# Semaphore head starts, filler products and the end of batch 0's scan in an eight-batch model kernel

## The reference, cut to what matters

```python
x = L0_attn_input_tensor                       # (8, 512, 128)
xn = _layernorm(x)
x = x + filter_0(xn) + moe_0(xn)
xn = _layernorm(x)
x = x + attention_1(xn) + moe_1(xn)
```

```python
u, res = split(xn @ in_proj_w.T)               # 256 channels each
u = silu(conv_b + 4-tap causal convolution of u)
dt, Bm, C = split(u @ x_proj_w.T)              # 8, 16 and 16 columns
delta = softplus(dt @ dt_proj_w.T + dt_proj_b)
h[t] = exp(delta[t] * A) * h[t-1] + delta[t] * Bm[t] * u[t]    # 16 states a channel
y[t] = sum over the states of h[t] * C[t]
m = ((y + u * D_skip) * silu(res)) @ out_proj_w.T
```

## Time and profile before

| | |
|---|---|
| median of 3 runs | 2461.3 us (2459.88 to 2467.54) |
| profiled execution, its own time | 2465.32 us |
| its span in the trace | 2463.2 us |
| mean granted TensorE clock | 0.904 |
| TensorE busy | 2038.7 us (83%) |
| VectorE busy | 1646.4 us (67%) |
| ScalarE busy | 1173.7 us (48%) |
| GpSimd busy | 958.8 us (39%) |

### The profile page before, as it was taken

One profiled execution on the slowest core, in us unless ns is written; L12 is line 12 of the kernel. 1 busy time (PEld: TensorE's weight loads), 2 busy tenths in 40 slices (PEclk: granted clock), 3 DMA queues, 4 the chain that ended last, 5 costly groups with the idle time before them and its releaser, 6 DMA issues.

```text
span 2463.2 us, 40604 instructions
## 1 busy us (share of the span) xinstructions
PE 2038.7 (83%) x12424; PEld 1295.3 (53%) x12424; DVE 1646.4 (67%) x2939; ACT 1173.7 (48%) x2703; POOL 958.8 (39%) x580
## 2 busy tenths in 40 slices
PE   4267888997899878998899888997789888988985
PEld 1033445664466545664466544664456644665564
DVE  3944786568865887658865788558866688644431
ACT  2223464345644466346643456345553456424631
POOL 1420583017810495007820387105840068303501
PEclk8567799988999999999999989999999889989997
DMA  2000012321213112321113112231123211132233
GB/s 105 0 18 0 27 46 71 117 78 38 89 66 111 57 46 69 112 91 46 60 67 122 63 48 79 78 101 58 42 69 116 85 46 56 69 127 74 73 114 112
DMA packets 82459, 175.18 MB, mean 71 GB/s; under 512 B 11448, under 2 KB 42560, under 8 KB 81984
## 3 DMA queue, kind: packets, MB, share of 16 engines
q1 hardware_dynamic: 78144, 164.05, 19.3%
q0 software_dynamic: 4096, 8.40, 1.1%
HBM read 123.71 MB, written 15.14 MB: 56 GB/s over the span
## 4 chain that ended last, share of the span: by engine, by line
PE 49%; DVE 17%; issue 15%; POOL 8%; ACT 5%; DMA 3%; SPq 1%; DVEq 0%; POOLq 0%; ACTq 0%
PE G L1049 5%; DVE HS L1564 4%; PE G L1065 4%; PE FM L1038 3%; DMA MW<-moe 3%; POOL Y L1998 3%; PE G L942 3%; PE G L953 3%; PE G L936 3%; PE FC L1026 2%; PE G L1087 2%; PE FM L906 2%; PE FC L1077 2%; POOL REG L2009 2%; POOL REG L2012 2%
## 5 line engine op out<-in xcount | busy, mean ns | idle before, releaser
L1564 DVE TENSOR_TENSOR_SCAN HS<-DA,D 128x1024 f32<-128x1024 f32 x128 | 351.0, 2742 | 15.0 <-ACT DA L1232 14.5
L1049 PE MATMUL G<-ident,REG 128*128 128x128 f32 x1280 | 242.9, 290 | 121.5 <-ACT SL L1361 79.4
L1998 POOL TENSOR_TENSOR Y<-Y,HC 128x1024 f32<-128x1024 f32 x114 | 280.4, 2460 | 144.7 <-DVE HC L1586 101.9
L2009 POOL TENSOR_TENSOR REG<-REG,cos_t 128x512 f32<-128x512 f32 x128 | 173.9, 1359 | 263.9 <-ACT REG L1334 263.7
L1049 PEld LDWEIGHTS G<-ident,REG 128*128 128x128 f32 x1280 | 149.3, 147 | 166.0 <-issue 147.4
L1038 PE MATMUL G<-REG 64*128 64x128 f32 (+3 forms) x768 | 221.4, 487 | 12.4 <-POOL REG L2012 11.3
L2012 POOL TENSOR_TENSOR REG<-REG 128x512 f32<-128x512 f32 x128 | 190.6, 1489 | 62.0 <-DMA REG<-ROT 54.9
L1350 ACT ACTIVATE REG<-G,maxes 128x128 f32<-128x128 f32 (+3 forms) x384 | 196.9, 513 | 25.8 <-DVE maxes L1865 24.9
L1232 ACT ACTIVATE DA<-DELTA,a_neg 128x511 f32<-128x511 f32 x256 | 180.9, 721 | 46.8 <-DVE HS L1564 46.7
L1865 DVE TENSOR_REDUCE maxes<-G 128x1 f32<-128x128 f32 (+3 forms) x384 | 165.6, 458 | 27.9 <-PE G L1041 27.9
L1559 DVE TENSOR_TENSOR D<-DU,FB 128x1024 f32<-128x1024 f32 x114 | 138.6, 1216 | 46.6 <-PE FB L796 43.5
(11 more groups left out here) (297 smaller groups left out, 4568.2 us busy)
## 6 DMA issues: line engine op xcount, KB each, us to landing
MW<-moe SPq DMA_DIRECT2D x120, 768.0 KB, 4.4
REG<-ROT SPq DMA_DIRECT2D x256, 128.0 KB
EW<-experts SPq DMA_DIRECT2D x16, 514.5 KB, 4.3
XG<-x_rows SPq DMA_DIRECT2D x8, 960.0 KB, 5.4
y_rows<-YO SPq DMA_DIRECT2D x120, 64.0 KB, 1.5
X<-xT SPq DMA_DIRECT2D x8, 256.0 KB, 5.9
W<-weights SPq DMA_DIRECT2D x1, 2048.0 KB, 9.4
REG<-xT SPq DMA_DIRECT2D x8, 256.0 KB, 2.6
```

Source lines behind the costliest of these rows:

```text
L1049: mm = pe.transpose(G[2][:, c * P:(c + 1) * P], PR[:, n % 2, c * P:(c + 1) * P], ident[:, :])
L1564: dve.tensor_tensor_scan(HS[:, :, :].rearrange("p h s -> p (h s)"), DA[:, n % 2, :, :].rearrange("p h s -> p (h s)"), D1[:, :, :].rearrang ...
L1998: pool.tensor_tensor(Y[:, :, :], Y[:, :, :], HC_EARLY if early else HC[:, n % 2, :, :], ALU.add).then_inc(y_add.sem, 1)
L2009: pool.tensor_tensor(rotated, rotated, cos_t[:, :], ALU.mult).then_inc(rope_d.sem, 1)
```

## The change

Four edits:
- SP raises only x_in's semaphore before the loads, the other 14 behind all ten first loads.
- TensorE raises three semaphores first (those that others wait for in their first step), and the 42 others in groups of 16, 16 and 10 behind steps p = 0, 1 and 2 of its front. VectorE does its four memsets before its 50 increments.
- Behind steps p = 3 to 10 TensorE multiplies the constants `avg` and `ones` 6, 2, 2, 2, 2, 4, 3 and 4 times into G[0]. Nobody reads the result, and nobody waits for these products.
- In batch 0 GpSimd does adds 0 to 14; the add of state 15 and the product with silu(res) are done by VectorE, behind its HC 15, with a wait for GpSimd's add 14. `front_end` stays in use for the other batches.

```diff
--- before.py
+++ after.py
@@ -564,8 +564,7 @@
 
         @block.sync
         def _(sp):
-            for s in by_sp:
-                s.head_start(sp)
+            x_in.head_start(sp)
             late = WEIGHTS["wq"][0]
             sp.dma_start(X[:, :], xT[0]).then_inc(x_in.sem, 16)
             for dst, src in ((conv_w[:, :, :], conv_rows.partition_broadcast(P)), (in_u, in_u_w), (ident[:, :], identity), (V_[:, :], vecs),
@@ -574,6 +573,10 @@
             for dst, src in ((W[:, 0:late], weights[:, 0:late]), (dt_lhs[:, :], dt_w), (causal_f, causal), (row_of_sb[:, :], row_of),
                              (row_bias[:, :], row_biases.partition_broadcast(P))):
                 sp.dma_start(dst, src).then_inc(s_const, 16)
+
+            for s in by_sp:
+                if s is not x_in:
+                    s.head_start(sp)
 
             sp.wait_ge(s_rows, 1)
             sp.dma_start(x_rows.rearrange("(p r) d -> p (r d)", p=P), REG[:, 0:4, :].rearrange("p k s -> p (k s)")[:, 0:MOE_TILES * D]).then_inc(s_rows, 16)
@@ -683,9 +686,16 @@
 
         @block.tensor
         def _(pe):
-            for s in by_pe:
+            first_waited = (n1.by_pe, dp_mm, r_mm)
+            others = [s for s in by_pe if s not in first_waited]
+            for s in first_waited:
                 s.head_start(pe)
             pe.wait_ge(s_made, 4)
+
+            def keep_warm(n):
+
+                for _ in range(n):
+                    pe.matmul(G[0][:, 0:P], avg[:, :], ones[:, :], start=True, stop=True)
 
             def bank(key, b, f):
 
@@ -1163,6 +1173,13 @@
                     elif p == 5:
                         pe.wait_ge(s_const, n_loads)
                     front_start(b, p, None)
+                    if p < 3:
+                        for s in others[16 * p:16 * (p + 1)]:
+                            s.head_start(pe)
+                    elif p < 11:
+                        keep_warm((6, 2, 2, 2, 2, 4, 3, 4)[p - 3])
+                for s in others[48:]:
+                    s.head_start(pe)
                 pe.wait_ge(s_made, 15)
                 for n in range(STATES):
                     front_b(b, n)
@@ -1426,12 +1443,12 @@
 
         @block.vector
         def _(dve):
-            for s in by_dve:
-                s.head_start(dve)
             dve.memset(avg[:, :], 1.0 / P).then_inc(s_made, 1)
             dve.memset(ones[:, :], 1.0).then_inc(s_made, 1)
             dve.memset(XN[:, 0:PAD], 0.0).then_inc(s_made, 1)
             dve.memset(DA[:, :, :, 0:1], 0.0).then_inc(s_made, 1)
+            for s in by_dve:
+                s.head_start(dve)
 
             def taps_made():
 
@@ -1943,6 +1960,14 @@
                     for part in range(3):
                         front_step(b, n, part, FB, FC)
 
+
+                dve.wait_ge(y_add.sem, y_add.at(b, STATES - 1))
+                dve.wait_ge(hc_mul.sem, hc_mul.at(b, STATES))
+                dve.tensor_tensor(Y[:, :, :], Y[:, :, :], HC[:, (STATES - 1) % 2, :, :], ALU.add).then_inc(y_add.sem, 1)
+                dve.wait_ge(y_add.sem, y_add.at(b))
+                dve.wait_ge(r_silu.sem, r_silu.at(b))
+                dve.tensor_tensor(Y[:, :, :], Y[:, :, :], SR[:, :, :], ALU.mult).then_inc(y_gate.sem, 1)
+
             def late():
 
                 dve.wait_ge(s_late, n_late)
@@ -2096,13 +2121,11 @@
                 front_skip(b)
                 front_du(b)
                 front_copy(b)
-                for n in range(STATES):
-                    if n + 1 < STATES:
-
-                        pool.wait_ge(scan_d.sem, scan_d.at(b, n + 2))
-                        pool.sem_inc(pool_passed, 1)
+                for n in range(STATES - 1):
+
+                    pool.wait_ge(scan_d.sem, scan_d.at(b, n + 2))
+                    pool.sem_inc(pool_passed, 1)
                     front_step(b, n)
-                front_end(b)
 
             def late():
```

## The result

The changed kernel takes 2450.19 us (median of 22 executions, 2425.95 to 2463.54), the kernel before beside it on the same chips 2460.59 us (22 executions, 2451.03 to 2473.97). The ratio is 0.9944 with the interval 0.9922 to 0.9966. It isn't the quotient of the two medians (0.9958); that of the two means lies within 0.0003 of it. Ratios leave out disturbed executions, one here (2463.54) and one of 2588.13 us in the first set with the fillers alone. On the median of 2461.3 us that the forecast started from, the ratio gives 2447.5 us (2442.1 to 2452.9). I had forecast 2454.3 with a range from 2449.9: the sign is right, the gain (13.8 us) is twice what I gave. Two more sets of the changed kernel, run later, gave 0.9956 and 0.9955, so the size isn't one lucky set.

What follows compares the result with a forecast made beforehand. The prediction took the start, front and scan of batch 0 as one serial chain, mostly TensorE and VectorE work plus issue time. Gains 4.1 + 2.2 + 1.0 - 0.3 = 7.0 us took 2461.3 to 2454.3 us, range 2449.9 to 2460.0.

Steps and rivals of the forecast that it cites:

- SP's order: Program start: 14 of SP's 15 increments move behind the loads, 0.9 us; X's load issued at 0.75, landed at 3.35.
- Rival 4: Program start: X lands at 6.65, so the start gains 1.2 us instead of 4.1; total 2457.2 us; chance 0.05.
- TensorE's and VectorE's order: Program start: first product at 3.4, mean subtracted at 5.95 instead of 10.02, VectorE being last; gain 4.1 us.
- Increments put off: Batch 0's front: TensorE's 42 postponed increments fit in its idle gaps and cost 0, with 0.9 us kept for the range.
- rival 3: Batch 0's front: increments wait for the products ahead of them, losing 0.9 us in two gaps; 2455.2 us; chance 0.10.
- End of the scan: Batch 0's scan: with last add and gate on VectorE, the `out_proj` product starts at 137.3 instead of 139.53; gain 2.2 us.
- Fillers: Batch 0's front: 0.3 us lost behind first taps, 1.0 gained by holding the clock for the second step-width product; net 0.7.
- rival 2: Batch 0's front: fillers hold nothing, second step-width product still takes 2.07 us; gain 6.0, total 2455.3 us; chance 0.17.
- Rival 1: First tap products of the front: clock rises sooner, up to 3.0 us more gain; total 2451.3 us; chance 0.20.
- The sum: Start, scan and front together: 4.1 + 2.2 + 1.0 - 0.3 = 7.0 us, moving everything from `out_proj` on earlier.

Runs made afterwards that it cites:

- the head starts alone: Kernel before with only the reordered increments (SP's 14, TensorE's 42, VectorE's memsets first), no fillers, scan end as before: 2458.35 us, ratio 0.999.
- cut kernels: Kernels shortened to batches 0 and 1, or 0 to 2, by leaving out the loop over later batches; with two batches the change gained 6.5 us in means.
- the cut to two batches: Kernel before, changed kernel, change without fillers and fillers alone, each with only batches 0 and 1; the change gained 6.5 us in means.
- neither cut: Two batches: fillers lowered the changed kernel's mean by 0.2 us, raised that of before by 0.3; three batches: 1024.79 us with fillers, 1022.1 without.

## Why the prediction was right and where it was wrong

**SP's order: right.** X's load went out at 0.81 (0.75 forecast) and landed at 3.61 (3.35), in 2.80 us. Rival 4, X late, is out.

**TensorE's and VectorE's order: right.** First product at 3.74 (3.4), subtraction at 5.93 (5.95), first taps at 15.85 (15.8). Which engine is last I had the wrong way round: 3.74 + 2.06 and 0.13 for the signal are 5.93, and with the product at 3.52 (the head starts alone) the subtraction follows at 5.71, so VectorE's increments end before that and not at 5.85, and TensorE sets the time. It cost nothing in the sum: the gain is 4.1 us, up to 4.4 in other executions.

**Increments put off: right.** The idle times of 2.98, 2.32 and 0.87 us are those of before to the hundredth; rival 3 is out.

**End of the scan: right.** 2.3 us, 2.2 forecast. VectorE added at 129.40 and gated at 130.66, and the centring of the next batch, pushed back to 131.80, made nobody wait.

**Fillers: the term had the wrong sign in the front.** I had +0.7, from a price of 0.3 us and a gain of 1.0. The price is 0.34 and 0.35 us in two pairs of traces, and can be more, as the second step-width product comes later against the clock's fall: from the subtraction to `out_proj` it is 126.1 to 126.5 us in the six traces with head starts, scan's end and fillers (cut kernels included) and 125.4 in the four with the first two alone. The gain isn't there: without fillers the second step-width product takes 1.12 to 1.22 us in six of seven traces of whole kernels (the first trace of before is the seventh), and with them it is slow in three of seven: the first of the change (1.90) and both of the fillers alone (1.86 and 2.07). The clock fell 20.5 us behind its rise in all of these but the first trace of before, fillers or not. I had read a cause, the gap, out of one fall, and that fall, 17.1 us behind the rise, was the odd one of twenty. Whether fillers would prevent just that odd one, one trace in ten without them can't show. The Trainium skill had spoken for this outcome ("TensorE: Matmul & The Clock Gate", section "Why this matters for your kernels"): only idle stretches longer than these cost a kernel its clock. By that rule the fillers give nothing here, and they gave nothing; but the clock did fall around products only 0.76 to 1.63 us apart, which it doesn't explain. So rival 2 has the right sum for the front, 6.0, but its condition (the product still takes 2.07) held in three of seven traces only; in the others it was fast, as it was without fillers.

**Rival 1, the clock rising sooner in the first taps: not borne out.** They took 5.46 us in the first trace after instead of 6.74, which looks like it. But over all traces they take 5.23 to 6.67 us (mean of 11: 5.97) where they start near 15.7, and 5.27 to 6.74 (mean of 9: 6.13) where they start at 19.9. That is luck of 1.5 us either way, and 0.16 us of difference.

**The sum.** 4.1 + 2.3 - 0.35 = 6.05 us in the front. The starts of `out_proj` are 132.0 to 132.4 in three traces of the change against 137.9, 138.0 and 139.5 in three of before: without the odd first trace 5.5 to 5.9 us, and 6.1 in the cut to two batches, whose whole gained 6.5. The sum of 7.0 was right within 1.5 us, its excess being the fillers' term. The prediction's "the front is the same in all of them" did not hold: it moved by 1.6 us between traces of before.

**The size of the whole: too small, and the cause of the rest stays open.** I wrote that from `out_proj` on every start is 7.0 earlier, apart from the clock. Pooled over three sessions, 45 executions of the change have a mean of 2447.8 us (standard error 1.3), all 167 of before 2459.8 (0.6), the 114 of the same three sessions 2459.0 (0.7): 11 to 12 us, of which the front holds 6 or a little more. The 5 us or so left lie behind `out_proj`. What they are I can't say. That the fillers make them was my best theory: without fillers the mean is 2454.9 (1.4, two sets), about the front's gain. A fit of my own to 295 executions of whole kernels, with a level for each session and one term for each part, gives 4.1 us to the head starts (1.4), 3.2 to the scan's end (1.5) and 4.2 to the fillers (1.2), which in the front only cost. The traces point to the same place, weakly: the seven attention stages add up to 1052.1 us (3.8) in the seven with fillers and 1060.9 (3.0) in the seven without, and their shortest length, 146.7 to 146.9, occurs in 7 of 42 stages of batches 1 to 6 with fillers and in none of 42 without. Against it: fillers alone gave -7.1 us in one set and +0.4 in the next, neither cut shows any effect of them, and no trace shows a way in which they would act so much later. Chance isn't excluded either, as two sets of before lie 3.7 and 4.4 us off their own like, though three sets of the change at -9.5 to -13.7 make it a thin explanation. Not tried: many more executions of the kernel without fillers, and fillers moved instead of removed.

**The step that failed** is, first, what the prediction put at nothing: "whatever leaves it moves all that follows to the left, the seven later batches included, and nothing there is shortened". Measured, the whole gained 11 to 12 us where the front gained about 6, so 5 or so came from stages to which the sum gave no term; their cause stays open, as said. Second, the fillers' term: +0.7 forecast, -0.35 or worse in the front, because the clock's fall follows its rise and not the gaps. Third, the range and its reason: "Medians of such runs also scatter: those of before span 2459.9 to 2467.5". Three executions were taken as the scatter, when the same kernel spans 2438 to 2475 and one stage alone moves by 8 us. With that seen (in the trace of before it could be: its attention stages run from 147.8 to 155.0), the lower end would have been some 4 us lower, by my estimate. That a measurement tells about 0.3% from no change was also too hopeful: sets of 12 give intervals of 0.2 to 0.3% to each side.

## What to carry to other kernels

Semaphore increments aren't free: before the first load or product they took their engine 0.06 (SP), 0.09 (VectorE) and 0.16 us (TensorE) each, by division of the time that the engine spent on them in the trace of before. TensorE's 45 set the start there; 42 of them behind its first steps, 14 behind SP's loads and VectorE's 50 beside the first load and product left no trace in the time. So look what an engine does before its first real work. One trace doesn't say why a clock fell: look whether the same gap holds the clock elsewhere, or in a second execution, before paying for fillers. Where repeated stages of one trace differ by several per cent, their standard deviation times the root of their number is an estimate of the scatter of the whole (here 7.6 us against 7.7 measured), and it tells how many executions a change of a few microseconds needs.

## What the runs showed of the hardware that was not expected

- The first stretch at 2.4 GHz began during the first tap products, anywhere from 3.1 to 6.2 us behind their start, and lasted 20.5 us in 19 of 20 traces of all kernels, those with the 25 filler products and those without (17.1 in the other).
- The granted clock can fall to 0.50 under a busy TensorE: in the first trace of the change near 39.9, 0.2 us into a product that stood 0.76 us behind work that filled 0.97 of a microsecond, and with 28 filler instructions ahead near 133.3, 1.4 us into the `out_proj` product. It held over 1.62 us of idleness in other executions.
- The same instructions of one attention stage take 146.7 to 155.1 us, in a few recurring lengths rather than evenly spread, with a granted clock from 0.97 to 0.92.
- A set of 12 executions of an unchanged kernel against 34 of the same kernel gave means of -3.7 and +4.4 us.
